# The first quarter's negated maxima go into the score banks as matrix products with diagonal blocks, and 19 maxima pairs, not 22, stand ahead of the first double step

## What is computed

```
x = x + layernorm(attention(layernorm(x)))          # 16 heads of 64
x = x + layernorm(ffn(layernorm(x)))                # 128 -> 32 -> 512 -> gelu -> 32 -> 128
attention: q = x Wq + bq, k = x Wk + bk, v = x Wv + bv; q = q / 8
           softmax(q k^T over the 2048 keys) v, then Wo and bo
```

## Time and profile before

| what | value |
|---|---|
| median of 3 runs | 2386.64 us (2386.33 to 2387.66) |
| the profiled execution's own time | 2388.58 us |
| its span in the trace | 2386.7 us |
| TensorE busy | 2348.6 us, 98% of the span |
| GpSimd busy | 2107.2 us, 88% |
| VectorE busy | 2035.4 us, 85% |
| ScalarE busy | 1415.4 us, 59% |
| mean granted clock of TensorE | 0.992 of 2.4 GHz |

### The profile page before, as it was taken

How to read it: one execution, slowest core, us unless ns; L and a number is a source line. 1 busy time by engine, 2 the same in 40 slices (tenths; PEclk the granted TensorE clock), 3 DMA queues, 4 the chain that set the end, 5 groups by cost and what they waited for, 6 DMA issues and landing times.

```text
span 2386.7 us, 43553 instructions
## 1 busy us (share of the span) xinstructions
PE 2348.6 (98%) x15628; PEld 1178.0 (49%) x15628; DVE 2035.4 (85%) x3208; ACT 1415.4 (59%) x1671; POOL 2107.2 (88%) x1206
## 2 busy tenths in 40 slices
PE   6999999999999999999999999999999999999998
PEld 3455454545445454454545445454544545444454
DVE  7888888888888888888888888888888888888877
ACT  5656556566565656656565655656656565655646
POOL 5888989888898989989888898989989888899986
PEclk8999999999999999999999999999999999999999
DMA  1100001000000000100001000100000000110101
GB/s 51 29 14 28 28 15 33 28 15 28 28 20 28 28 15 28 34 15 27 28 16 32 28 19 23 33 23 20 28 27 20 28 28 15 35 30 21 37 27 36
DMA packets 62969, 62.55 MB, mean 26 GB/s; under 512 B 28868, under 2 KB 46660, under 8 KB 62756
## 3 DMA queue, kind: packets, MB, share of 16 engines
q1 hardware_dynamic: 61748, 59.44, 8.5%
q10 hardware_dynamic: 1008, 0.33, 0.1%
HBM read 56.88 MB, written 2.61 MB: 25 GB/s over the span
## 4 chain that ended last, share of the span: by engine, by line
PE 94%; DVE 2%; POOL 1%; DMA 1%; ACT 1%; issue 1%; SPq 0%; POOLq 0%; DVEq 0%; ACTq 0%
PE o_ps L442 37%; PE spare_ps L401 14%; PE score_ps L421 10%; PE score_ps L427 10%; PE score_ps L424 10%; PE spare_ps L387 3%; PE spare_ps L487 3%; PE spare_ps L378 3%; PE spare_ps L369 3%; PE spare_ps L454 1%; DVE max_part L867 1%; POOL total L1142 1%; DMA m_all<-m_scratch 0%; DVE ln_stats L835 0%; PE spare_ps L467 0%
## 5 line engine op out<-in xcount | busy, mean ns | idle before, releaser
L1142 POOL TENSOR_TENSOR total<-total,probs 128x832 f32<-128x832 f32 (+1 forms) x896 | 1761.0, 1965 | 232.6 <-ACT probs L691 161.1
L867 DVE TENSOR_REDUCE max_part<-spare_ps 128x1 f32<-128x512 f32 x2027 | 1303.6, 685 | 295.3 <-PE spare_ps L401 276.7
L691 ACT ACTIVATE probs<-score_ps 128x1024 f32<-128x1024 f32 x1024 | 999.2, 1021 | 785.4 <-PE score_ps L427 784.2
L442 PE MATMUL o_ps<-probs,v_sb 128*64 128x512 f32 x4096 | 977.2, 598 | 0.0
L442 PEld LDWEIGHTS o_ps<-probs,v_sb 128*64 128x64 f32 x4096 | 268.3, 136 | 434.7 <-issue 282.5
L401 PE MATMUL spare_ps<-k_hi,q_hi 64*128 64x512 f32 x2027 | 466.2, 454 | 6.9 <-DVE max_part L867 3.2
L401 PEld LDWEIGHTS spare_ps<-k_hi,q_hi 64*128 64x128 f32 x2027 | 195.2, 184 | 436.8 <-issue 262.1
L421 PE MATMUL score_ps<-q_hi,kd_hi 64*128 64x512 f32 x2048 | 406.9, 393 | 0.9 <-ACT score_ps L681 0.9
L427 PE MATMUL score_ps<-q_hi,kd_lo 64*128 64x512 f32 x2048 | 405.2, 392 | 0.0
L424 PE MATMUL score_ps<-q_lo,kd_hi 64*128 64x512 f32 x2048 | 403.8, 390 | 0.0
L903 DVE TENSOR_REDUCE part_sum<-probs 128x192 f32<-128x768 f32 (+1 forms) x255 | 392.4, 1539 | 0.8 <-ACT probs L691 0.7
(11 more groups left out here) (136 smaller groups left out, 1118.5 us busy)
## 6 DMA issues: line engine op xcount, KB each, us to landing
m_all<-m_scratch SPq DMA_DIRECT2D x64, 512.0 KB, 4.4
denom<-denom_scratch SPq DMA_DIRECT2D x122, 128.0 KB, 2.9
m_scratch<-neg_rows SPq DMA_DIRECT2D x256, 1.0 KB
y_acc<-in_L_attn_x SPq DMA_DIRECT2D x8, 256.0 KB, 6.6
key_f<-in_L_attn_x SPq DMA_DIRECT2D x8, 256.0 KB, 2.8
block_out<-probs SPq DMA_DIRECT2D x8, 256.0 KB, 2.3
denom_col<-denom SPq DMA_DIRECT2D x61, 4.0 KB
denom_scratch<-denom_col SPq DMA_DIRECT2D x61, 4.0 KB, 1.4
```

Source lines behind the costliest of these rows:

```text
L442: last = nc.tensor.matmul(o_ps[half(h), :], v_sb[:, b, kt, half(h)], probs[:, st % RING, h, :], start=(kt == 0), stop=(kt == T - 1))
L691: nc.scalar.activation(probs[:, st % RING], score_ps[st % 2][:], ACT.Exp, scale=SCALE).then_inc(s["exp_done"], 1)
L867: nc.vector.reduce_max(max_part[:, G % 2, h, qt, kc:kc + 1], bank[max_bank(n, h)], AX.X).then_inc(s["max_done"], 1)
L1142: nc.gpsimd.tensor_tensor(others(total[:, G % 2], G), so_far, others(probs[:, st % RING], G), ALU.add).then_inc(s["sum_done"], 1)
```

## The change

Pairs ahead of the loop fall from 22 to 19. Doubles 0, 1 and 2 then do three pairs each (one ahead of the scores, two behind them), and from double 3 on all is as before. The diagonal blocks: VectorE writes four blocks `ident * neg_max` of 128 x 128 for head 0, ScalarE four for head 1, both into `m_all`. TensorE multiplies a stationary matrix of ones (128 x 64) by them, twice for each bank (upper and lower 64 partitions), for four banks: eight products of 128 x 512. ScalarE's two first seeds, VectorE's first transpose and SyncE's first five DMAs go. The fourth key projection moves from behind pair 6 to behind pair 8, the second query projection to behind pair 9, the values' bias to behind pair 11, the sixth group of transposes (counted from 0) from behind pair 17 to behind the seeds, and the seventh from behind pair 18 into double 0, behind its third pair.

```diff
-LEAD = 22
+LEAD, FIRST = 22, 19
+def maxima_from(n):
+    return min(FIRST + 3 * n, LEAD + 2 * n, STEPS)
+def maxima_in(n):
+    return range(maxima_from(n), maxima_from(n + 1))
...
-        FIRST_LATE_X = {13: 4, 15: 5, 17: 6, 18: 7}
-        FIRST_MAX_BANKS = [("r0", "r1"), ("s00", "s01")] * (T // 2 + 1) + [("s10", "s11"), ("r0", "r1"), ("o", "r2"), ("r0", "r1")]
+        FIRST_LATE_X = {13: 4, 15: 5}
+        FIRST_MAX_BANKS = [("r0", "r1"), ("s00", "s01")] * (T // 2) + [("r0", "r1"), ("o", "r2"), ("r0", "r1")]
+        FIRST_V_DONE = 11
...
+            def first_seed(self, st):
+                self.pe.wait_ge(s["diag_done"], 2)
+                for h in range(2):
+                    ps = self.take(f"s{st}{h}", None, 0)
+                    for k in range(2):
+                        last = nc.tensor.matmul(ps[half(k), :], ones[:], m_all[:, h, :], start=True, stop=True)
+                last.then_inc(s["seed_done"], 1)
...
-            me.max_pair(6)
-            me.project_k(0, 3, FIRST_K_BANK[3])
-            for n in range(7, LEAD):
+            for n in range(6, FIRST):
                 me.max_pair(n)
                 if n == 8:
+                    me.project_k(0, 3, FIRST_K_BANK[3])
+                if n == 9:
                     me.project_q(1, FIRST_Q_BANK[1])
                 if n == 10:
                     me.project_v(0, 0, TC, FIRST_V_BANK)
                 if n in FIRST_LATE_X:
                     me.transpose_x(FIRST_LATE_X[n])
+                if n == FIRST - 2:
+                    me.first_seed(0)
+                    me.first_seed(1)
+                    me.transpose_x(6)
             for n in range(DOUBLES):
...
-                if 2 * n + LEAD < STEPS:
-                    me.max_pair(2 * n + LEAD)
+                for m in maxima_in(n)[:1]:
+                    me.max_pair(m)
                 me.scores(2 * n)
                 me.scores(2 * n + 1)
-                if 2 * n + LEAD < STEPS:
-                    me.max_pair(2 * n + LEAD + 1)
+                for m in maxima_in(n)[1:]:
+                    me.max_pair(m)
+                if n == 0:
+                    me.transpose_x(7)
...
+        def act_diag(act):
+            act.wait_ge(s["neg_max_done"], 1)
+            act.wait_ge(s["const_ready"], 1)
+            for t in range(TC):
+                ins = nc.scalar.activation(m_all[:, 1, t * P:(t + 1) * P], ident[:], ACT.Copy, scale=neg_max[:, 0, TC + t:TC + t + 1])
+            ins.then_inc(s["diag_done"], 1)
...
+            act_xnT(act, 5)
+            act_diag(act)
             act_x(act, 6)
-            act_xnT(act, 5)
             act_x(act, 7)
             act_xnT(act, 6)
             act_xnT(act, 7)
-            act_seed(act, 0)
-            act_seed(act, 1)
...
+        def dve_diag(dve):
+            dve.wait_ge(s["neg_max_done"], 1)
+            dve.wait_ge(s["const_ready"], 1)
+            nc.vector.tensor_tensor(m_all[:, 0, :].rearrange("p (t n) -> p t n", t=TC), ident[:].unsqueeze(1).to_broadcast([P, TC, P]),
+                                    neg_max[:, 0, 0:TC].unsqueeze(2).to_broadcast([P, TC, P]), ALU.mult).then_inc(s["diag_done"], 1)
...
                 if n == T - 1:
                     dve_neg_max(dve, 0)
-                if n == T:
+                    dve_diag(dve)
+                if n == FIRST_V_DONE:
                     dve_v(dve, 0, 0, TC, FIRST_V_BANK)
...
-            sp_m_out(sp, 0)
-            sp_m_back(sp, 0)
```

More of the change, by code:

```diff
@@ L124, in spare_banks @@
         G, u, c, d = n // PER_CHUNK, n // (PER_CHUNK * NC), n // PER_CHUNK % NC, n % PER_CHUNK
-        for st in (2 * n + LEAD, 2 * n + LEAD + 1):
-            for h in range(2 if st < STEPS else 0):
-                use("max", 2 * st + h)
+        for m in maxima_in(n):
+            for h in range(2):
+                use("max", 2 * m + h)
         if keys_at(u, c, d):
@@ L669, in act_q @@
                                  bias=b_qk[:, G // (B * NC) % 2, 0:1]).then_inc(s["q_hi_done"], 1)
+        def act_diag(act):
[4 more added lines that the diff above has]
+            ins.then_inc(s["diag_done"], 1)
         def act_seed(act, st):
             G = st // T
[L674 to L680, removed]
+            act.wait_ge(s["exp_done"], st - 1)
+            act.wait_ge(m_dma[G % 2], m_back_count(G))
             nc.scalar.activation(score_ps[st % 2][:], m_all[:], ACT.Copy).then_inc(s["seed_done"], 1)
@@ L867, in dve_max, with m_back_count @@
             nc.vector.reduce_max(max_part[:, G % 2, h, qt, kc:kc + 1], bank[max_bank(n, h)], AX.X).then_inc(s["max_done"], 1)
+        def dve_diag(dve):
[3 more added lines that the diff above has]
+                                    neg_max[:, 0, 0:TC].unsqueeze(2).to_broadcast([P, TC, P]), ALU.mult).then_inc(s["diag_done"], 1)
+        def m_back_count(G):
+            return 16 * (G // 2 + G % 2)
         def dve_neg_max(dve, G):
@@ L874, in dve_neg_max @@
                                     negate=True).then_inc(s["neg_max_done"], 1)
+            if G == 0:
+                return
             dve.wait_ge(s["neg_max_done"], G + 1)
-            if G >= 2:
-                dve.wait_ge(s["m_out"], 64 * (G - 1))
+            if G >= 3:
+                dve.wait_ge(s["m_out"], 64 * (G - 2))
             nc.vector.transpose(neg_rows[:, G % 2, :], neg_max[:, G % 2, :]).then_inc(s["neg_rows_done"], 1)
@@ L1048, in dve_program @@
                 dve_x_statistics(dve, g)
-            for n in range(LEAD):
+            for n in range(FIRST):
                 for h in range(2):
@@ L1057, in dve_program @@
                 G, u, c, d = n // PER_CHUNK, n // (PER_CHUNK * NC), n // PER_CHUNK % NC, n % PER_CHUNK
[L1058 to L1061, removed]
+                for m in maxima_in(n)[:1]:
+                    dve_max(dve, m, 0)
+                    dve_max(dve, m, 1)
                 for g in ffn_at(n, LOW):
@@ L1069, in dve_program @@
                     dve_recip(dve, G - 1)
-                if more:
-                    dve_max(dve, 2 * n + LEAD + 1, 0)
-                    dve_max(dve, 2 * n + LEAD + 1, 1)
+                for m in maxima_in(n)[1:]:
+                    dve_max(dve, m, 0)
+                    dve_max(dve, m, 1)
                 if d == NEG_MAX_AT and G + 1 < CHUNKS:
@@ L1292, in sp_m_out @@
         def sp_m_out(sp, G):
-            sp.wait_ge(s["neg_rows_done"], G + 1)
-            if G >= 2:
-                sp.wait_ge(m_dma[G % 2], 16 * (G // 2))
+            sp.wait_ge(s["neg_rows_done"], G)
+            if G >= 3:
+                sp.wait_ge(m_dma[G % 2], m_back_count(G - 2))
             for b in range(P // 32):
@@ L1300, in sp_m_back @@
         def sp_m_back(sp, G):
-            if G:
-                sp.wait_ge(s["seed_done"], 2 * G)
-            sp.wait_ge(s["m_out"], 64 * (G + 1))
+            sp.wait_ge(s["seed_done"], 2 * G)
+            sp.wait_ge(s["m_out"], 64 * G)
             sp.dma_start(m_all[:].rearrange("p h n -> p (h n)"),
```

4 lines of the change are left out of this document (2 added, 2 removed).

## The result

The changed kernel takes 2391.69 us (median of 22 runs, 2390.12 to 2394.57) against 2387.11 us for the kernel before, run beside it (22 runs, 2386.31 to 2390.54). The ratio is 1.0019, with a 95% interval of 1.0013 to 1.0025: 4.6 us slower, where 4.0 was forecast. The median lies 1.1 us above the forecast 2390.6 and inside the range of 2386.0 to 2394.0. It is just inside the 0.2% that I had called "same", though the interval reaches beyond that. The profiled execution took 2392.06 us (span 2390.4); I had expected 2392.6 for a like one.

What follows compares the result with a forecast made beforehand. TensorE was taken to bound the kernel behind the front, so only double 3's start counted: 0.53 + 3.45 = 4.0 us on 2386.64 gave a median of 2390.6 us, range 2386.0 to 2394.0.

Steps and rivals of the forecast that it cites:

- the sum: Double 0 0.53 us later plus doubles 0 to 2 3.45 us longer: 4.0 us in all.
- The bound: Behind the front TensorE sets the pace, so a shift of double 3's start is not made up later.
- The front: Work ahead of double 0: hole closed, three pairs fewer, seeds on TensorE; double 0 starts 0.53 us later.
- Pair 15 done: VectorE's last reduction before the maximum would end at 37.8 us, against 38.24 before, with the bias already done.
- The ScalarE term: ScalarE's four scaled copies for the diagonals, taken as 1.64 us like L745, done at 39.7.
- Doubles 0 to 2: From pair 19's product to double 3: 19.56 us against 16.11, so 3.45 later.
- the bank wait: Third pair in doubles 0 to 2 goes 1.33 us after the last product, not 0.23: 1.10 lost, three times.
- The exponentials: In double 1, scores 2 and 3 wait for exponentials behind ScalarE's copy of group 7: 0.7 us.
- the removed hole: VectorE's 2.52 us hole before pair 7 closes, about 2 us won, spent on the seeds and pair 18.
- first rival: Clock stays low longer at the seeds and bank waits of doubles 0 to 2: 2.8 us more, 2393.4; chance 0.27.
- second rival: Clock is up for the seeds: done at 43.24, 1.8 us earlier, 2388.8; chance 0.18.
- third rival: Third pair is free: pairs 20 to 27 hide behind other TensorE work, 2385.9; chance 0.12.

Runs made afterwards that it cites:

- e13: The changed kernel unchanged, measured again for a second profile: 2392.57 us, +5.3 against the kernel before.
- e0: The kernel before unchanged, measured again for a second profile: 2387.06 us.
- e3: The changed kernel with ScalarE taking the first exponential ahead of its copy of transposed group 7: 2390.50 us.
- e5: The kernel before with only the changed kernel's order of key projection, query projection and values' bias in the front: 2387.90 us.
- e6: The changed kernel with its seeds by products, but 22 pairs ahead of double 0 and two pairs in every double: 2391.79 us.
- e7: The changed kernel with 19 pairs ahead and third pairs, but seeds by the round trip and ScalarE as before: 2391.43 us.
- e4: The changed kernel with added products that nobody reads behind each of pairs 11 to 16: 2390.60 us.
- e1: The changed kernel with the three pairs of doubles 0 to 2 standing apart among scores and projections: 2391.31 us.
- e2: The changed kernel with pair 18 between the seeds of the two banks instead of behind them and the transposes: 2389.66 us.
- e12: e5 with added products that nobody reads behind pairs 11 to 19 and behind pair 21: 2385.31 us.
- e11: e10 with e4's added products behind pairs 11 to 16: 2386.59 us.
- e10: The changed kernel with pairs 18 to 20 between the seed products, 21 pairs ahead, and e3's order on ScalarE: 2388.96 us.

## Why the prediction held

The forecast was 4.0 us and the median 4.6, but that closeness is partly luck. Profile against profile the front lost 3.1 us, 0.9 less than the sum, because both of its terms were too high. The other 1.5 us of the median (2.2 in e13) come from elsewhere, and the next paragraph has what the traces say of it.

**The bound.** That TensorE paces all behind double 3, so that a shift there stays, was right in the main: the seeds of the second chunk come 3.17 us later than before, and those 2000 us later 2.6. In the last five chunks the shift went from 2.6 to 1.5, then to 4.1 and 3.8 (ScalarE's seeds at 2113, 2186, 2259 and 2298 us of the kernel before). The dip belongs to that profile of the kernel before, since e0 shows it against it too (from 2.0 to 3.3 us earlier, then 1.9). Part of the rise is the stay at half clock near 2231: e13, without it, goes from 2.2 to 3.5 and 3.4. So the stay costs some 1.3 us, and I had taken the tail as fixed. My base was also a profile whose clock had gone like the changed kernel's; against e0's the same front is 4.3 later. In how many of the runs the clock goes which way isn't known, so what makes up the rest of the median stays open.

**The front.** Pair 15 done: 37.8 forecast, 38.13 found, since the fourth key projection began at 25.63 and not 25.40 and took 1.91 to the next product and not 1.74, so that pair 9 and all behind it came 0.3 to 0.4 late. Seeds from 39.8, found 39.71. Done at 45.04, found 44.58: the clock was back 2.6 us after they began, not 3.6. Double 0 0.53 later, found 0.17. The ScalarE term was mis-sized: four diagonal copies took 1.28 us, not the 1.64 of L745, whose copies have two pointer operands. That hid the late pair 15: the copies were done at 39.65, for 39.7. The estimate by the Trainium skill ("ScalarE: Activation LUTs", "What ACT_TABLE_LOAD costs") had been 0.37 less, 1.27; here the page was nearer than the nearest row. VectorE's product took 0.69, like the bias.

**Doubles 0 to 2.** Forecast 19.56, found 19.01 and 19.06 (19.08 from 47.14 to the 66.22 of the chain; the forecast's 16.11 has its ends from these two views as well, and is 16.04 in the table). The mechanism was right and the sizes a little high. For the bank wait I had 1.33 us from product to product; the trace has 1.29, 1.27 and 1.27 (48.84 to 50.13, 54.54 to 55.81, 60.78 to 62.05). The idle 0.88 of the rows stands behind the product's own 0.40, so it compares with 1.33 and not with the 1.10 lost. VectorE begins 0.43 to 0.45 us behind a pair that follows the scores, where I had taken 0.54 from a pair that stands alone. The values go 0.51 and 0.50 behind the last pair, for 0.60. The exponentials cost 0.6 (e3), for 0.7. Together the doubles were 0.5 us too high and the front 0.4.

**What the sum didn't say.** I listed the removed hole and the three pairs as gains spent on the seeds. e5, e6 and e7 show it more sharply: closing the hole wins nothing by itself, and neither half of the change is good alone.

**The rivals.** The clock fell again in double 0 in e4 and e6, as in the first rival, behind gaps of 1.47 us and of up to 1.24 us, but not in the changed kernel's own profiles, where it was granted in full from 42.3 us to at least 2230. So it did not happen in the change, and the bank waits of 0.88 us didn't bring it down. The rule of the Trainium skill that I had weighed ("TensorE: Matmul & The Clock Gate", on a second failure mode) doesn't agree with the change itself, and whether it is what acts in those two isn't shown. The clock was low at the seeds (second rival out), and the third pair was not free (third rival out; e1).

## What to carry to other kernels

Work put on the engine that runs in order costs what is queued behind it: here the seeds' own 4.9 us hid behind nothing because pair 18 stood behind them, and moving that one pair won 1.6 us (e2). When a loop deals a few banks in turn, a third user in one turn pays the reader's latency, about 1.05 us each time here (1.27 to 1.29 from product to product, where 0.23 would do), and spreading the users gave back a third of it (e1). Where TensorE waits ahead of dense work, products that nobody reads may be worth more than a shorter chain: 1.6 us behind the maximum in e12, with 1.9 in the median that its interval doesn't settle, and none in e4, where the clock fell again right behind them. And compare profiles from a common event: here the clock ahead of the maximum differed from profile to profile by 1 to 1.5 us, as much as most edits moved.

## What the runs showed of the hardware

The clock: with added products it stayed at 2.4 GHz up to double 0 (e4, e11, e12), where all eleven other profiles have it at half for 6.8 to 17.1 us from 33.6 to 39.7 us on. In e11 and e12 it stayed up in double 0 as well; in e4 it was at half there from 45.4 to 48.8 us. The kernel before met different stretches at half clock in its two profiles, from 25 and 35 us on in one, only from 39.7 in the other; the changed kernel met the same ones twice. The seed products took 4.94, 6.31 and 6.19 us in executions of one and the same order of TensorE's work (changed kernel, e3, e6). Near 2230 us, where all kernels run the same code, the changed kernel, e1, e2, e4, e5, e6, e10 and e11 show 3 to 4 us at half clock, and the two profiles of the kernel before, e3, e7, e12 and the second of the changed kernel show none. Between the two profiles of the changed kernel that is worth some 1.3 us, with no edit at all.
